# One core, first node stage: VectorE's expert mask placed one turn later and behind the next tile's negative part

## What is computed

```python
x = x + _L0_gnn_ref(_layernorm(x), edge_index, W_l, W_r, att, bias)   # ends in elu(out) + x
router_logits = xf @ Wr + br                  # xf: the layer norm of x
topk_logits, topk_idx = jax.lax.top_k(router_logits, 1)
for e in range(8):
    h = relu(xf @ W1[e] + b1[e])              # 32 wide
    oe = h @ W2[e] + b2[e]
    out = out + where(topk_idx == e, gate * oe, 0.0)    # gate: softmax of one value, so 1
x = x + out
```

## Time and profile before

| what | value |
|---|---|
| time, median of 3 executions | 2936.8 us |
| lowest and highest | 2929.69 and 2940.85 us |
| the profiled execution, its own time | 2943.63 us |
| its span, first to last instruction | 2941.9 us |
| mean granted TensorE clock | 0.885 |
| VectorE busy over the span | 1821.7 us (62%) |
| POOL busy over the span | 1789.1 us (61%) |
| TensorE matmuls over the span | 2220.5 us (75%) |

### The profile page before, as it was taken

The page is one execution under the profiler, slowest core; times in us unless marked ns, Lnnn a source line. Parts: engine busy times, 40 slices in busy tenths (PEclk is TensorE's granted clock), DMA queues, the critical chain, the costliest instruction groups (busy, mean ns, idle before and its releaser), DMA issues. The chain is left out here.

```text
span 2941.9 us, 43922 instructions
## 1 busy us (share of the span) xinstructions
PE 2220.5 (75%) x11763; PEld 1308.8 (44%) x11789; DVE 1821.7 (62%) x5128; ACT 920.2 (31%) x2016; POOL 1789.1 (61%) x2143
## 2 busy tenths in 40 slices
PE   8999999857777728999978859999992677773000
PEld 3444444335555516666644436666661344442000
DVE  4776766524444459999921126777774477666666
ACT  1111111024445415777753315555552000000000
POOL 4555555566666348888536624777775555553776
PEclk9999999969898959999989979999996699897555
DMA  6655555468888646788669956666751799995999
GB/s 204 223 189 180 190 185 181 145 191 249 255 258 267 206 142 198 255 264 262 206 210 353 361 185 204 213 215 215 215 176 44 224 366 363 341 307 196 346 374 340
DMA packets 361398, 698.60 MB, mean 237 GB/s; under 512 B 51609, under 2 KB 85235, under 8 KB 361153
## 3 DMA queue, kind: packets, MB, share of 16 engines
q1 hardware_dynamic: 239672, 399.69, 40.0%
q0 software_dynamic: 76720, 217.93, 23.8%
q10 hardware_dynamic: 44761, 78.17, 7.5%
HBM read 426.08 MB, written 287.17 MB: 242 GB/s over the span
## 5 line engine op out<-in xcount | busy, mean ns | idle before, releaser
L2085 POOL DMA_INDIRECT xg<-n_rows,ids x219 | 218.3, 997 | 158.7 <-PE psum L154 81.1
L148 PE MATMUL psum<-wl,xT 128*128 128x512 f32 x632 | 288.8, 599 | 0.0
L148 PE MATMUL psum<-wg,yT 128*128 128x512 f32 x632 | 286.7, 597 | 0.0
L148 PE MATMUL psum<-wr,xT 128*128 128x512 f32 x632 | 284.1, 592 | 0.0
L2235 POOL DMA_INDIRECT q<-slot_outputs,qs x158 | 173.4, 1097 | 86.7 <-issue 47.9
L337 ACT ACTIVATE xb<-xa,xsc 128x512 f32<-128x512 f32 x79 | 64.2, 814 | 480.7 <-POOL xsc L397 480.6
L1637 POOL DMA_INDIRECT slot_tokens<-sl x158 | 169.1, 1070 | 66.0 <-issue 60.4
L154 PE MATMUL psum<-ident,xg 128*128 128x128 f32 x876 | 152.3, 308 | 71.6 <-issue 34.1
L384 POOL TENSOR_TENSOR ve<-mv,epst 128x1 f32<-128x1 f32 x79 | 51.0, 645 | 254.1 <-DVE mv L439 254.1
L2173 DVE COPY gT<-psum 128x512 f32<-128x512 f32 x219 | 142.0, 685 | 101.3 <-PE psum L154 54.2
L684 POOL DMA_INDIRECT gl<-xl_rows,idx x118 | 129.9, 1101 | 112.5 <-DVE vv L736 65.1
(11 more groups left out here) (320 smaller groups left out, 5497.2 us busy)
## 6 DMA issues: line engine op xcount, KB each, us to landing
slot_outputs<-yo ACTq DMA_DIRECT2D x54, 1024.0 KB
x_rows<-x SPq DMA_DIRECT2D x158, 256.0 KB
edge_sums<-eo SPq DMA_DIRECT2D x29, 1056.0 KB
edge_sums<-go SPq DMA_DIRECT2D x29, 1024.0 KB
xT<-in_xTt SPq DMA_DIRECT2D x79, 256.0 KB
xl_rows<-xl SPq DMA_DIRECT2D x79, 256.0 KB
xr_rows<-xr SPq DMA_DIRECT2D x79, 256.0 KB
residual_rows<-xb SPq DMA_DIRECT2D x79, 256.0 KB
```

The source lines that it names most:

```text
L148: last = nc.tensor.matmul(ps, lhs[:, k, :], rhs[:, k, :], start=(k == 0), stop=(k == DK - 1))
L2085: pool.indirect_dma_start(xg[:, t % 8, :], None, XN3, bass.IndirectOffsetOnAxis(ids[:, t:t + 1], 0), bounds_check=NP - 1, oob_is_err=False ...
```

## The change

`routed` gets lag 12 in place of 11 and stands behind `negative`, ahead of `best`. Every step that uses its result, and every step behind those, gets a lag one higher: `turn_h`, `down`, `copy_h`, `add_experts`, `minus_mean2`, `spread2`, `root2`, `slopes`, `shifts`, `shifts_up`, `scaled` and both stores. `x1` gets an eleventh row. `hb` and `hm` keep two.

```diff
-        x1 = sb("x1", [P, 10, D], F32, pc)
+        x1 = sb("x1", [P, 11, D], F32, pc)
...
-                tiles_in_turn(NT, ((0, load), (16, store_x2), (26, store_g)))
+                tiles_in_turn(NT, ((0, load), (17, store_x2), (27, store_g)))
...
-                tiles_in_turn(NT, ((3, average), (9, pairwise(root1)), (6, pairwise(minus_mean1)), (15, fourwise(minus_mean2)),
-                                    (20, fourwise(root2)), (1, later_rows)))
+                tiles_in_turn(NT, ((3, average), (9, pairwise(root1)), (6, pairwise(minus_mean1)), (16, fourwise(minus_mean2)),
+                                    (21, fourwise(root2)), (1, later_rows)))
...
-                    if t >= 10:
-                        dve.wait_ge(c_x2, t - 9)
-                        dve.wait_ge(c_tr1, t - 9)
-                        dve.wait_ge(c_sq, t - 9)
+                    if t >= 11:
+                        dve.wait_ge(c_x2, t - 10)
+                        dve.wait_ge(c_tr1, t - 10)
+                        dve.wait_ge(c_sq, t - 10)
...
-                    (11, hidden), (5, negative), (0, once(larger, 0)), (21, fourwise(slopes)), (11, best), (2, listed_part),
-                    (0, once(below, 0)), (21, fourwise(shifts)), (11, its_number), (2, self_part),
-                    (0, once(edge_share, 1)), (21, fourwise(shifts_up)), (11, number_f), (4, positive),
-                    (0, once(weight_sum, 1)), (11, one_hot), (0, once(inverse, 1)), (14, add_experts), (11, routed),
+                    (11, hidden), (5, negative), (12, routed), (0, once(larger, 0)), (22, fourwise(slopes)), (11, best), (2, listed_part),
+                    (0, once(below, 0)), (22, fourwise(shifts)), (11, its_number), (2, self_part),
+                    (0, once(edge_share, 1)), (22, fourwise(shifts_up)), (11, number_f), (4, positive),
+                    (0, once(weight_sum, 1)), (11, one_hot), (0, once(inverse, 1)), (15, add_experts),
                     (0, once(shares, 1))))
...
-                tiles_in_turn(NT, ((8, turn1), (9, up), (12, turn_h), (13, down)))
+                tiles_in_turn(NT, ((8, turn1), (9, up), (13, turn_h), (14, down)))
...
-                tiles_in_turn(NT, ((4, exp_of), (8, spread1), (0, exp_group), (12, copy_h), (19, spread2), (8, copy1),
-                                   (25, scaled)))
+                tiles_in_turn(NT, ((4, exp_of), (8, spread1), (0, exp_group), (13, copy_h), (20, spread2), (8, copy1),
+                                   (26, scaled)))
```

More of the change, by code:

```diff
@@ L1204, in negative @@
                     dve.wait_ge(c_ex, t + 1)
-                    if t >= 10:
-                        dve.wait_ge(c_x2, t - 9)
-                        dve.wait_ge(c_tr1, t - 9)
-                        dve.wait_ge(c_sq, t - 9)
+                    if t >= 11:
+                        dve.wait_ge(c_x2, t - 10)
+                        dve.wait_ge(c_tr1, t - 10)
+                        dve.wait_ge(c_sq, t - 10)
                     if t >= 12:
                         dve.wait_ge(c_nm, t // 2 - 5)
-                    nc.vector.scalar_tensor_tensor(x1[:, t % 10, :], mi[:, t % 2, :], 1.0, xq[:, t % 2, :],
+                    nc.vector.scalar_tensor_tensor(x1[:, t % 11, :], mi[:, t % 2, :], 1.0, xq[:, t % 2, :],
                                                    ALU.min, ALU.add, accum_out=sum1(t, 0)).then_inc(c_x1, 1)
@@ L1259, in add_experts @@
                     dve.wait_ge(c_dn, t + 1)
-                    nc.vector.scalar_tensor_tensor(x2[:, t % 12, :], bank[3 + 4 * (t % 2)], 1.0, x1[:, t % 10, :],
+                    nc.vector.scalar_tensor_tensor(x2[:, t % 12, :], bank[3 + 4 * (t % 2)], 1.0, x1[:, t % 11, :],
                                                    ALU.mult, ALU.add, accum_out=sum2(t, 0)).then_inc(c_x2, 1)
@@ L1295, in turn1 @@
                         pe.wait_ge(c_x1T, t - 1)
-                    tr4(bank[4 * (t % 2)], x1[:, t % 10, :]).then_inc(c_tr1, 1)
+                    tr4(bank[4 * (t % 2)], x1[:, t % 11, :]).then_inc(c_tr1, 1)
                 def up(t):
@@ L1355, in spread1 @@
                         act.wait_ge(c_sq, t - 1)
-                    act.activation(sq[:, t % 2, :], x1[:, t % 10, :], ACT.Square, bias=sum1(t, 1),
+                    act.activation(sq[:, t % 2, :], x1[:, t % 11, :], ACT.Square, bias=sum1(t, 1),
                                    accum_out=sum1(t, 2)).then_inc(c_sq, 1)
```

## The result

| | before | after |
|---|---|---|
| median of 15 executions each, same chip | 2934.66 us | 2945.84 us |
| ratio after to before, 95% interval | | 1.0037 (1.0026 to 1.0048) |
| VectorE, POOL, TensorE busy in the profiled execution | 1821.7, 1789.1, 2220.5 | 1827.7, 1786.1, 2208.4 |
| `hidden` of the first tile to `hidden` of the last (timeline) | 383.6 us | 392.9 us |
| from there to the end of the last `gs` | 403.4 less 383.6 = 19.8 us | 22.0 us |

The change costs 0.37%, some 11 us (2934.66 x 0.0037 = 10.9), where a gain of 7.8 was forecast. The time lies inside the range; the direction is wrong. The stage explains all of it: its first `hidden` to its last `gs` is 11.5 us longer, 9.3 of it in the middle and 2.15 at the end.

What follows compares the result with a forecast made beforehand. VectorE, always busy mid-stage, was taken as the bound: 18.08 + 0.06 + 0.06 + 1.00 + 0.26 = 19.46 us a cycle against 20.08, 10.1 gained less 2.3 at the end, so 2936.8 to 2929.0 us; range 2914 to 2947.

Steps and rivals of the forecast that it cites:

- The mask at 0.42: VectorE's mask (`routed`), 877 ns on average before, was to take its plain 0.42 us in nearly all turns.
- `negative` at 0.75 in C and D: Turns C and D (T mod 4 = 3, 0): `negative` held 0.20 us by POOL's sum, net cost 0.06 each.
- `shares` taking the mask's 0.26: Turn T mod 4 = 1: `shares`, behind `add_experts`, takes over the mask's 0.26 us hold, so no gain there.
- The longer end: Stage's end: one more turn, filled only by `turn_h` and `down`, was to cost 2.3 us.
- 13 / 4 x 0.62: VectorE's cycle of four turns was to take 19.46 us against 20.08, 0.62 less a cycle.
- Either way one long hold a cycle, which I take as 1.00.: Turn T mod 4 = 1: POOL's late sum holds `negative` or `listed_part` once a cycle, net 1.00 us.
- The sum unchanged: `slopes`, `shifts`, `shifts_up`, some 0.26 us together, move from turn D (T mod 4 = 0) to A (1); cycle total unchanged.
- a `one_hot` held in every B: Range's slow end, 2947 us: `one_hot` held 1.08 us more in each turn B (T mod 4 = 2).
- Priced 0, cover thin: `one_hot` now needs TensorE's `turn_h` of the same turn; margin 0.41 us, some 0.2 in places, cost taken as 0.
- 18.08: VectorE's cycle of four turns without the mask's holds: 18.08 us, from 20.08 less 2.00.
- Rival 3: POOL gets the port between `positive` and `one_hot`, holding `one_hot` 1.08 us more; 2946 to 2977 us, chance 0.12.
- Rival 1: POOL's sum in time: the 1.00 hold becomes 0.06, cycle 18.52, execution 2914 us; chance 0.22.

Runs made afterwards that it cites:

- e1: Mask alone moved (`routed` lag 12, behind `negative`), all other lags as before, against the kernel before: ratio 0.9984 (0.9972 to 0.9996).
- e2: The changed kernel with the mask back in its old place, so only the lags and the eleventh `x1` row change: ratio to before 1.0069 (1.0046 to 1.0091).
- e6: The changed kernel with the power in `root2` replaced by a multiplication with 1: ratio to before 1.0003 (0.9988 to 1.0017).
- e10: e9 with `weight_sum` placed ahead of `number_f` and `positive`: ratio to before 1.0001 (0.9989 to 1.0012).
- e5: The changed kernel with three `hm` buffers and `shifts_up` moved behind `add_experts`: ratio to before 0.9994 (0.9978 to 1.0011).
- e4: The changed kernel with `shifts_up` moved from ahead of `positive` to behind `add_experts`: ratio to before 1.0013 (0.9998 to 1.0028).
- e15: The changed kernel unedited, run again on another chip beside the kernel before: ratio 1.0043 (1.0025 to 1.0061).
- e3: The changed kernel with three `hm` buffers, so `one_hot` needs the transposes of the turn before again: ratio to before 1.0023 (1.0011 to 1.0035).
- e11: The changed kernel with POOL's gathers given out 0, 2, 1, 1 over T mod 4 = 0 to 3: ratio to before 0.9984 (0.9971 to 0.9996).
- e13: e9 with `minus_mean1` and `minus_mean2` moved from POOL to ScalarE: ratio to before 0.9955 (0.9940 to 0.9971).
- e7: The changed kernel with POOL's gather moved from the end of its turn to right behind the sum: ratio to before 1.0027 (1.0010 to 1.0044).
- e9: e1 with POOL's gathers given out 1, 2, 1, 0 over T mod 4 = 0 to 3: ratio to before 0.9972 (0.9959 to 0.9985).

## Why the prediction was wrong

**What was right.** The mask at 0.42: in all 79. `negative` at 0.75 in C and D (0.74 to 0.76), where no sum is late: as worked out from the 1.01 of 1.21 us. `shares` taking the mask's 0.26: 0.48 in place of 0.21 in T = 17 and 21 and in most cycles of e1. The longer end: 2.15 against 2.3. The bound: VectorE's list, held through the shared path.

**What agrees by luck.** The first 13 turns gained 1.9 us, and 13 / 4 x 0.62 = 2.0 was the forecast. But `root2` doesn't run there yet, so the long hold of the forecast was missing, and three holds of `one_hot` in D (1.35 where 0.28 is plain) stood in its place. And the time lies inside the range, whose slow end came from a `one_hot` held in every B; what came was another set of holds of about that size.

**The step that failed: "Either way one long hold a cycle, which I take as 1.00."** Three things in it.

- *The size of the hold.* It took `negative` as held for the sum's 1.21. It is held until the sum is over, from its own earlier start: 2.24, that is 1.56 more than plain. The working decided by who starts first; in after, e1, e2, e6 and e10 VectorE started first by 0.1 to 0.6 us and lost. It is also later than worked out: from a sum's end (1296.52 + 1.75) to the next sum's start (1303.08) it is 4.81 us, not 4.44, since POOL's small steps last longer there: `root1` ends 1.48 behind the sum instead of the 1.14 of the earlier trace rows, and `root2`'s power takes 1.57 instead of 1.46, while the gather behind them is shorter (1.11 instead of 1.34).
- *"The sum unchanged" for the group steps.* True for the durations. But `shifts_up` shifts `positive` by 0.08, from 0.05 ahead of the sum's start to 0.03 behind it, and `weight_sum` is held for 1.12 in eleven of twelve cycles (three of twelve in e5, six in e4). Nothing in the prediction asked which short instruction stands behind `positive` in turn A.
- *That the cycle stays a cycle of four.* A long A leaves TensorE idle, and then the next term can fail.

**"Priced 0, cover thin" for the new wait of `one_hot`.** The margin of 0.41 was there in ordinary turns: no wait in B and C of 4.23 and 4.30. It assumed TensorE at its pace. After an idle time of 2.70 us `up` took 1.44 longer than in the earlier trace rows, and the wait came. Where `up` kept its 2.02 (five of eight times in e15), it didn't. e3 prices it: 5.0 us in the profiled execution, 2.4 against e15. It is a follower: e11 keeps the wait and never meets it.

So for the long form of a cycle, in the prediction's own terms: 18.08 + 0.06 + 0.06 + 1.56 (late sum) + 1.12 (`weight_sum`, in place of 0.26 at `shares`) = 20.88, and 20.87 is what e3 shows in ten of twelve cycles and e15 in four. In the change the waits behind the low clock make it 21.28.

**The rivals.** Rival 3, POOL getting the path earlier, was the right family with the wrong place: it named `one_hot` in B, and without a wait that happened only in the first cycles, in D (1.35 three times). Its other way there, `one_hot` waiting briefly for `turn_h`, did come: in C at T = 51 it waits 0.13 and is then held, 1.14. Its own bound was good: it "decides the sign from 0.48 us a cycle on", and the cycle lost 0.8 to 1.2. Rival 1, POOL in time, is what e13 brings about, though with the old lags: 18.52 was worked out, 18.53 came. The Trainium skill (SBUF — State Buffer, "SBUF: two separate sides") has it that whoever starts first gets the port for its whole instruction. The prediction doubted that rule in one direction; the rows of after contradict it in the other as well, if recorded starts are starts.

The chances were too sure of the sign for what they rested on: a tie between two starts that nothing in the trace of before settled.

**What stays open.** What holds VectorE before the sum's recorded start: the gather ahead of it, or the sum's claim already made while it waits. e7 has no hold of 2.2 without the gather, but has one of 1.54. What decides `weight_sum`: at the same recorded distances it is held in some cycles and free in others (the two cycles of e13 above; T = 29 of the change against the other eleven), so no distance of the trace separates them. Why the clock falls behind some idle times of 2.70 us and not behind others. And e13's missing microseconds.

## What to carry to other kernels

A helper engine's operation that shares a path with the bounding engine does its harm by when it is due. Add up that engine's turn, with its small steps as long as the trace shows them beside the bounding engine, and see in which turn it goes over; steps that run every second and every fourth turn fall together in other turns as soon as one lag moves by one. Moving a held instruction can move the hold to the next candidate (`negative`, mask, `weight_sum`, `positive` and `one_hot` took it in turn). Making the helper punctual removed the long hold of `negative` (e9, e11), but that of `weight_sum` only in nine of twelve cycles of e13. And a shift of lags is a change of its own: try it apart from the move that it serves.

## What was not expected of the hardware

- An instruction of VectorE with two SBUF inputs, recorded as started 0.11 to 0.58 us before POOL's sum, was held until the sum had ended: 1.95, 2.06, 2.24, 2.42 us. Beside a gather whose next sum wasn't due yet, such instructions ran free (`negative` 0.68 in B of after, beside the gather of 1310.16).
- 0.08 us in the place of one instruction changed how often `weight_sum` took 1.30 instead of 0.18: eleven of twelve cycles in e3, three of twelve in e5. No recorded distance foretold the single cycle.
- The same 2.70 us without a matmul were followed by an `up` of 3.46 us at a granted clock of 0.50 in the change, and by one of 2.02 in e15 at 1178.82. In the change all six such gaps were followed by a slow `up`, in e15 three of eight, in e3 four of eight.
- POOL's indirect gather took 1.00 (e10) to 1.75 us (e2), and its 128x4 power 1.08 (T = 44 of the change) to 1.57.
